# Expert rows turned by the DMA, pad rows written earlier, and dense rows loaded from ScalarE's queue

## The chip, the cores and the metric

The kernel runs on one core of one Trainium2 chip. The metric is the device time in microseconds (us), the median of three runs: 1864.76 us for the kernel before, with runs from 1861.49 to 1867.23. Lower is better. One further execution was profiled; it took 1854.92 us, of which the trace spans 1853.1 us.

## The reference, cut to what matters

One transformer layer, on x of 4 sequences of 1024 tokens with 256 features: latent attention with 16 heads, and then a mixture of experts beside a shared expert.

```python
x = x + attention(layernorm(x))               # 16 heads, causal, latent keys and values
h = layernorm(x)                              # the rest, per token of 4096
scores = softmax(h @ gate_w.T)                # 16 experts
topk_w, topk_idx = top_k(scores, 2)
combine = sum(one_hot(topk_idx) * topk_w)     # weights of the two experts of a token
gu = einsum('th,ehj->etj', h, w_gate_up)      # 2 x 176 columns per expert
y = einsum('eti,eih,te->th', silu(gate) * up, w_down, combine)
y = y + swiglu(h @ shared_gate_up) @ shared_down
x = x + y
```

A token needs only its two experts, so the kernel computes 8192 rows of expert work instead of 65536.

## The kernel before, in words

The 4096 tokens are 32 tiles of 128 rows. `section(t)` is the attention of tile t on every engine, t from 0 to 31, with side jobs of its neighbours between the units of the softmax: the projections of tile t + 2, the output projection of tile t - 1, and the shared expert and the router of tile t - 2. Two sections more (32 and 33) have no attention and finish the tiles 30 and 31. The order of the work on each engine is written out by hand (`SIDE`, `due`); engines meet at semaphores alone.

An operand of 32 bits is split into two f16 parts, high and low, and a product is three f16 products. So a row of an expert's input is 512 f16 numbers (256 high, 256 low).

The router picks two experts for each token. There is a list in HBM (`lists`) for each expert, and GpSimd scatters the normalized rows of a tile to the lists of their experts (`scatter`, two indirect DMAs per tile). A row of a list is 514 f16 numbers, 1028 bytes: the 512 of the input, and a 32-bit number that says to which row of `y_exp` the result belongs. `used` holds the next free row of each list; VectorE advances it in `places(q)`, and at the last tile it copies it to integers (`free_i`, semaphore `used_ready`).

A list does not end at a multiple of 128 rows, so pad rows are written behind each list: `write_pads` writes one tile of 128 pad rows at the free row of each of eight lists, once on SyncE (SP) and once on ScalarE (ACT), and SP writes one tile more to a dummy list. This is after section 33. SP then waits for the pads, for the scattered rows and for a table `tab`, which tells for each of 80 tiles of expert rows where it starts and whose it is.

The expert phase goes over these 80 tiles, eight in a round of the loop (`Fori`). For tile n, SP reads the start row into a register (`value_load`) and loads the tile into one of eight buffers (`xg`, semaphore `xg_in`). TensorE (PE) turns the four blocks of 128x128 with the identity (`xg_transposes`), ScalarE copies them from PSUM (`xg_copy`), PE multiplies with gate and up (`expert_up`), ScalarE and VectorE make the hidden rows, PE turns them (`h_transposes`), VectorE copies, PE multiplies with down (`expert_down`), ScalarE copies (`y_copy`) and GpSimd scatters the rows to `y_exp` (`send`). PE's order in step n is h_transposes(n), expert_up(n + 2), xg_transposes(n + 4), expert_down(n). SP loads tile n + 8 when the result of tile n has left (`m_out`), since the indices of the scatter lie in the same buffer.

Between its first eight loads and the loop SP also loads 4 MB of `dense`, the sum of x and the shared expert, for the last phase, in which VectorE adds the two weighted results of each token and the rows are stored.

SP issues in attention, too: the turns of queries, keys, outputs and hidden rows by DMA, the loads of x and the stores of `dense`. For section 32 these are, in this order, `load_residual(31)`, `turn_output(31, 1)` (half of the turned attention output of tile 31, which the output projection on PE waits for), `turn_hidden(30)`, `turn_x2(31)` and `store_dense(30)`.

Of the kernel before, what the change touches and what calls it, by code (L numbers as in the profile page):

```python
# [135 lines left out]
def build(nc, x, wqaT, wqb_peT, wqb_nopeT, wkva, wkT, wvT, wo, gateT, wgu, wd, wsg, wsd,  # L136
# [3 lines left out]
    with ctx:  # L140
# [3 lines left out]
        def sem(name):  # L144
# [105 lines left out]
                   m_xT m_xTs m_gu m_gate m_q m_hid m_hi m_lo m_hT m_hTs m_down m_y  # L250
# [10 lines left out]
        xg_in = [sem(f"xg_in{k}") for k in range(8)]  # L261
        m_out = [sem(f"m_out{k}") for k in range(8)]
# [59 lines left out]
        xg, w_at = carve(work, 0, (XB, ROW), F16)  # L322
        pT_mem = pT[:, 0, :, :, :].rearrange("p a g n -> p (a g n)").bitcast(F32)
        xgT, p_at = carve(pT_mem, 0, (2, 2, KD, P), F16)
        m_hs, p_at = carve(pT_mem, p_at, (2, 2, I_E), F16)
# [39 lines left out]

        def write_pads(eng, half):
            rows = nc.values_load_multi_w_load_instructions(free_i[0:1, half * E // 2:(half + 1) * E // 2],
                                                            engines=[eng.engine], min_val=0, max_val=DUMMY - P)[1]
            for row in rows:
                eng.dma_start(lists[ds(row, P), :], pad[:, :]).then_inc(s.pads, 16)  # L370
# [3 lines left out]
        def _(sp):  # L374
# [226 lines left out]
        def _(pe_):  # L601
# [231 lines left out]
            def xg_transposes(n, q, par, m):  # L833
                pe_.wait_ge(xg_in[q], m * 16 + 16)
                for a in range(2):
                    for k in range(KD):
                        last = pe_.transpose(tt[par][:, (2 * a + k) * P:(2 * a + k + 1) * P],  # L837
                                             xg[:, q, a * D + k * P:a * D + (k + 1) * P], id16[:, :])
                last.then_inc(s.m_xT, 1)

# [3 lines left out]
            def expert_up(n, par, e):  # L844
                pe_.wait_ge(s.m_xTs, n + 1)
                split_product(s_ps[:, par, 0:2 * I_E], lambda a, k: xgT[:, par, a, k, :],
                              lambda b, k: wgu_sb[:, k, ds(e, 1), b, :], list(range(KD))).then_inc(s.m_gu, 1)
# [30 lines left out]
            xg_transposes(0, 0, 0, 0)  # L878
            xg_transposes(1, 1, 1, 0)
            expert_up(0, 0, held_expert(0))  # L880
            xg_transposes(2, 2, 0, 0)
            expert_up(1, 1, held_expert(1))
            xg_transposes(3, 3, 1, 0)

            nc.disable_value_cache = False
            with pe_.Fori(0, NMT // XB - 1) as m:
                e = [held_expert(k) for k in range(3)]
                for q in range(XB):
                    n = m * XB + q
                    h_transposes(n, q % 2)  # L890
                    expert_up(n + 2, q % 2, e[q + 2])
                    if q + 3 < XB:
                        e.append(expert_of(n + 3))
                    else:

                        read_expert(n + 3, q + 3 - XB)
                        e.append(held_expert(q + 3 - XB))
                    xg_transposes(n + 4, (q + 4) % XB, q % 2, m + (q + 4) // XB)
                    expert_down(n, e[q])
            nc.disable_value_cache = True  # L900
            e = [held_expert(k) for k in range(3)]
            for q in range(XB):
                n = NMT - XB + q
                h_transposes(n, n % 2)
                if n + 2 < NMT:
                    expert_up(n + 2, n % 2, e[q + 2])
                if n + 3 < NMT:
                    e.append(expert_of(n + 3))
                if n + 4 < NMT:
                    xg_transposes(n + 4, (n + 4) % XB, n % 2, (n + 4) // XB)  # L910
                expert_down(n, e[q])
# [3 lines left out]
        def _(act):  # L915
# [193 lines left out]

            act.wait_ge(s.used_ready, 1)  # L1110
            write_pads(act, 1)


# [4 lines left out]

            def xg_copy(n, par):
                act.wait_ge(s.m_xT, n + 1)  # L1120
                copy(xgT[:, par, :, :, :].rearrange("p a k n -> p (a k n)"), tt[par][:, 0:4 * P]).then_inc(s.m_xTs, 1)
# [14 lines left out]
            xg_copy(0, 0)  # L1136
            xg_copy(1, 1)
            expert_gate(0, 0)
            xg_copy(2, 0)
            expert_gate(1, 1)  # L1140
            xg_copy(3, 1)
# [27 lines left out]
        def _(dve):  # L1169
# [203 lines left out]
            def places(q):  # L1373
# [153 lines left out]
            def section(t):  # L1527
                for k in range(units(t)):
                    side(t, k, 0)
                    prob_lo(t, k, 0)  # L1530
                    side(t, k, 1)
                    maxima_ahead(t, k)
                    prob_lo(t, k, 1)
                    if shifted(t % TB, k):
                        shifted_sums(t, k)
                    side(t, k, 2)
                    side(t, k, 3)
                    search(t, k)
                    if (t, k) == (4, 2):
                        expert_scales()  # L1540
                side(t, units(t), 0)
                search(t, "end")
# [4 lines left out]
            dve.memset(pad[:, 0:2 * D], 0.0)  # L1547
            dve.memset(pad[:, 2 * D:ROW].bitcast(I32), 2 * NY)
# [84 lines left out]
        def _(pool):  # L1633
# [70 lines left out]
            def scatter(q):  # L1704
# [60 lines left out]
            def send(n, q):  # L1765

                pool.wait_ge(s.m_y, n + 2)
                own_wait(pool)
                pool.indirect_dma_start(y_exp, bass.IndirectOffsetOnAxis(xg[:, q, 2 * D:ROW].bitcast(I32), 0), m_ys[:, q % YB, :],  # L1769
                                        None, bounds_check=NY - 1, oob_is_err=False).then_inc(m_out[q], 16)  # L1770
            with pool.Fori(0, NMT // XB) as m:
                for q in range(XB):
                    send(m * XB + q, q)
# [47 lines left out]
```

## Time and profile before

| | us |
|---|---|
| median of 3 runs | 1864.76 |
| the profiled execution | 1854.92 |
| its span in the trace | 1853.1 |
| attention sections, to the last output turn | 0 to 1546.9 |
| end of tiles 30 and 31 | 1546.9 to 1580.2 |
| pads, until the first load of expert rows | 1580.2 to 1596.7 |
| expert phase | 1596.7 to 1810.2 |
| combination | 1810.2 to 1853.1 |

Over the span PE is busy 84%, VectorE 71%, ScalarE 56% and GpSimd 53%. The share of an engine is a mean over these stages; what a change of one stage is worth is read from the rows of that stage. Times in the rows are us from the start of the span. "SPq" and "ACTq" are the sequencers of SP and ScalarE, on which DMAs are issued; the duration of a DMA row is what the issue took, and "to landing" runs from the issue to the completion. The names of buffers in the trace are those of the memory that they share: `xg` is `work`, the pad row is `x_sb`, `dense_sb` is `weights`, and `m_ys` is `probs`.

### The profile page before, as it was taken

To read this page: it belongs to the slowest core of one execution; us is meant where nothing else is said; L and a number is where in the kernel's file an instruction comes from. 1 tells how busy PE (TensorE), PEld (TensorE's weight loads), DVE (VectorE), ACT (ScalarE), POOL (GpSimd) and SP (SyncE) were. 2 spreads that over 40 slices of the span, in tenths; PEclk is the share of its full clock that TensorE was granted. 3 is DMA by queue.
4 is the path that set the end of the run, shared out by engine and by line. 5 is a ranking of instruction groups with operands and counts; after the bars stand their busy time and mean duration, and the time that the engine had idled before them with its cause. 6 is when DMAs were issued, how large, how long until landed. Compare 5 with 4: busy or idle time off the path is not lost.

```text
span 1853.1 us, 46010 instructions
## 1 busy us (share of the span) xinstructions
PE 1553.7 (84%) x16418; PEld 1100.7 (59%) x16419; DVE 1311.5 (71%) x2964; ACT 1028.9 (56%) x2344; POOL 978.4 (53%) x1580
## 2 busy tenths in 40 slices
PE   8765888999879999998799999888999995399980
PEld 3243566766656767666567666666667663266650
DVE  1365877788777877878687788768878884255556
ACT  1243565666656666665566666656666662266650
POOL 3024567655477776554777666557766423134440
PEclk9787899999999999999899999999999997699995
DMA  6337532212235333213533323234432111733327
GB/s 163 86 98 111 84 70 58 50 31 53 58 76 107 64 61 61 52 22 73 98 65 65 57 58 59 52 72 85 87 58 52 31 20 38 186 92 104 102 73 272
DMA packets 333653, 143.96 MB, mean 78 GB/s; under 512 B 277168, under 2 KB 328403, under 8 KB 333398
## 3 DMA queue, kind: packets, MB, share of 16 engines
q1 hardware_dynamic: 311584, 108.68, 29.5%
q10 hardware_dynamic: 14966, 15.88, 3.1%
q0 software_dynamic: 6912, 16.83, 2.7%
q8 instruction: 123, 2.02, 0.4%
q14 instruction: 68, 0.56, 0.1%
HBM read 46.78 MB, written 29.53 MB: 41 GB/s over the span
## 4 chain that ended last, share of the span: by engine, by line
PE 49%; DVE 20%; ACT 7%; issue 6%; DMA 5%; SPq 4%; POOL 3%; DVEq 1%; ACTq 0%; POOLq 0%
PE of_ps L603 23%; PE s_ps L603 14%; PE t_ps L759 10%; DVE pT L1485 5%; DVE smax L1456 3%; ACT pT L917 2%; SPq L427 2%; DVE smax L1460 2%; ACT probs L1041 1%; DVE nmax L1464 1%; DVE nmax L1467 1%; DMA y_exp<-probs,work 1%; DVE work L1291 1%; PE t_ps L837 1%; ACT probs L1046 1%
## 5 line engine op out<-in xcount | busy, mean ns | idle before, releaser
L1485 DVE TENSOR_TENSOR pT<-t_ps,pT 128x512 f16<-128x512 f32 (+3 forms) x688 | 409.7, 598 | 181.2 <-ACT pT L917 177.9
L917 ACT CAST pT<-t_ps 128x512 f16<-128x512 f32 (+3 forms) x688 | 354.6, 515 | 283.3 <-PE t_ps L759 282.1
L603 PE MATMUL s_ps<-kT,qT 128*128 128x512 f16 (+3 forms) x2304 | 491.9, 328 | 7.8 <-DMA kT<-ks_sb 4.3
L759 PE MATMUL t_ps<-id,probs 128*128 128x128 f32 x2304 | 382.9, 281 | 67.1 <-ACT probs L1041 26.6
L759 PEld LDWEIGHTS t_ps<-id,probs 128*128 128x128 f32 x2304 | 257.7, 142 | 167.9 <-issue 77.2
L1041 ACT ACTIVATE probs<-s_ps,nmax,fac 128x640 f32<-128x640 f32 (+3 forms) x256 | 269.1, 1051 | 1.9 <-DVE nmax L1464 1.9
L603 PE MATMUL of_ps<-weights,xT 128*128 128x512 f16 (+1 forms) x960 | 221.1, 370 | 56.6 <-DVE ks_sb L1280 22.5
L603 PEld LDWEIGHTS of_ps<-ckv,pT 128*128 128x128 f16 x6912 | 242.1, 98 | 43.0 <-DVE o_sb L1319 10.4
L603 PE MATMUL of_ps<-ckv,pT 128*128 128x64 f16 x6912 | 259.0, 194 | 8.0 <-DVE o_sb L1319 7.7
L603 PEld LDWEIGHTS s_ps<-kT,qT 128*128 128x128 f16 x2304 | 218.3, 99 | 76.1 <-issue 5.9
L603 PEld LDWEIGHTS of_ps<-weights,xT 128*128 128x128 f16 x960 | 83.3, 102 | 146.5 <-DVE ks_sb L1280 25.8
L1456 DVE TENSOR_REDUCE smax<-s_ps 128x1 f32<-128x512 f32 (+1 forms) x256 | 157.3, 648 | 4.1 <-PE s_ps L603 3.8
L1769 POOL DMA_INDIRECT y_exp<-probs,work x80 | 78.7, 984 | 148.9 <-ACT probs L1134 147.8
L1680 POOL TENSOR_TENSOR os_<-o_sb,os_ 128x512 f16<-128x512 f32 x60 | 70.1, 1168 | 161.7 <-ACT os_ L917 152.5
L1046 ACT ACTIVATE probs<-s_ps,nmax,fac 128x256 f32<-128x256 f32 (+3 forms) x224 | 144.2, 651 | 0.3 <-DVE nmax L1467 0.3
L1438 DVE TENSOR_REDUCE smax<-s_ps 128x1 f32<-128x768 f32 (+2 forms) x136 | 122.8, 903 | 12.8 <-PE s_ps L603 12.2
L603 PE MATMUL of_ps<-weights,oT 128*128 128x256 f16 x768 | 99.6, 292 | 25.1 <-DMA oT<-os_ 23.0
L1664 POOL TENSOR_TENSOR work<-work,sin_sb 128x544 f32<-128x544 f32 x60 | 95.2, 1586 | 45.9 <-ACT work L917 28.6
L603 PE MATMUL s_ps<-maskbf,idbf 128*128 128x128 bf16 x512 | 113.3, 221 | 0.0
L603 PEld LDWEIGHTS of_ps<-weights,oT 128*128 128x128 f16 x768 | 78.5, 104 | 43.0 <-issue 25.6
L1460 DVE TENSOR_REDUCE smax<-s_ps 128x1 f32<-128x512 f32 (+2 forms) x160 | 94.7, 627 | 5.6 <-PE s_ps L603 5.3
L603 PE MATMUL s_ps<-wgu_sb,pT 128*128 x480 | 86.8, 318 | 0.0
(210 smaller groups left out, 2428.8 us busy)
## 6 DMA issues: line engine op xcount, KB each, us to landing
work<-lists SPq DMA_DIRECT2D x80, 128.5 KB, 2.0
wgu_sb<-wgu ACTq DMA_DIRECT2D x2, 2816.0 KB, 10.9
x_sb<-x SPq DMA_DIRECT2D x32, 128.0 KB, 2.5
x<-x SPq DMA_DIRECT2D x32, 128.0 KB, 2.4
dense<-den SPq DMA_DIRECT2D x32, 128.0 KB, 2.7
weights<-dense SPq DMA_DIRECT2D x1, 4096.0 KB, 16.7
qT<-y_exp SPq DMA_DIRECT2D x16, 256.0 KB, 5.6
work<-y_exp SPq DMA_DIRECT2D x16, 256.0 KB, 7.0
```

Source lines behind the costliest of these rows:

```text
L603: return pe_.matmul(o, a, b, start=start, stop=stop)
L759: last = pe_.transpose(t_ps[:, h, c * P:(c + 1) * P], probs[:, u % 2, g * L + j * P:g * L + (j + 1) * P], id32[:, :])
L917: return act.copy(o, i)
L1041: act.activation(probs[:, par, 0:L], s_flat[:, 1024 * par:1024 * par + L], ACT.Exp, bias=nmax[:, par, 0:1], scale=f_att, accum_out=ssum[:, ...
L1046: last = act.activation(probs[:, par, g * L:(g + 1) * L], s_flat[:, base:base + L], ACT.Exp, bias=nmax[:, par, g:g + 1], scale=f_att, accu ...
L1438: dve.tensor_reduce(smax[:, par, 0:G], view, AX_X, ALU.max).then_inc(s.maxs, 1)
L1456: last = dve.tensor_reduce(smax[:, par, h:h + 1], bank[:, 0:(j1 - j0) * P], AX_X, ALU.max)
L1460: last = dve.tensor_reduce(smax[:, par, h * n:(h + 1) * n], view, AX_X, ALU.max)
L1485: dve.tensor_tensor(pT[:, u % 2, 1, h, 0:w], t_ps[:, h, 0:w], pT[:, u % 2, 0, h, 0:w], ALU.subtract).then_inc(s.lo_p, 1)
L1664: st_.do(pool.tensor_tensor(rot2[:, :, k:ROPE:2], pe_of(n)[:, :, 1 - k:ROPE:2], sin_b, ALU.mult))
L1680: pool.tensor_tensor(os_[:, 1, :], o_sb[:, :], os_[:, 0, :], ALU.subtract).then_inc(s.lo_o, 1)
L1769: pool.indirect_dma_start(y_exp, bass.IndirectOffsetOnAxis(xg[:, q, 2 * D:ROW].bitcast(I32), 0), m_ys[:, q % YB, :], None, bounds_check=NY ...
```

## The change

There are three parts.

- The rows of an expert tile come turned. SP issues a DMA transpose of 128 rows x 512 numbers out of `lists` in HBM into `xgT`, and a second DMA for the 4 bytes per row of the index (`m_rows`, new semaphores `rows_in`). `xg_transposes` on PE and `xg_copy` on ScalarE are gone. `expert_up` waits for `xg_in`, `send` for `rows_in`.
- The pads are written from the state after tile 29, in which a list may grow by at most 256 rows more, so that each list gets three tiles (384 rows) of pads. SP writes all of them, after its section 31. `free_i` is made in `places(29)`. The scatter of tile 30 on GpSimd waits until all pads have landed. VectorE makes the pad row at the start of section 30.
- `dense` is loaded from ScalarE's queue, ahead of its first `expert_gate`.

```diff
+        xgT, w_at = carve(work, 0, (XB, 2 * KD, P), F16)
+        m_rows, w_at = carve(work, w_at, (XB, 2), F16)
+        PADS = 3
             for row in rows:
-                eng.dma_start(lists[ds(row, P), :], pad[:, :]).then_inc(s.pads, 16)
+                eng.dma_start(lists[ds(row, PADS * P), :].rearrange("(p c) n -> p c n", c=PADS),
+                              pad.unsqueeze(1).broadcast_to([P, PADS, ROW])).then_inc(s.pads, 16)
 @block.sync
-            for t in range(NT + 2):
+            for t in range(NT):
                 section(t)
             sp.wait_ge(s.used_ready, 1)
-            write_pads(sp, 0)
+            for half in range(2):
+                write_pads(sp, half)
             sp.dma_start(lists[DUMMY:DUMMY + P, :], pad[:, :]).then_inc(s.pads, 16)
+            for t in range(NT, NT + 2):
+                section(t)
             def expert_rows(n, q):
                 row = sp.value_load(tab[0:1, 0, ds(n, 1)], min_val=0, max_val=DUMMY)
-                sp.dma_start(xg[:, q, :], lists[ds(row, P), :]).then_inc(xg_in[q], 16)
+                sp.dma_start_transpose(xgT[:, q], lists[ds(row, P), 0:2 * D]).then_inc(xg_in[q], 16)
+                sp.dma_start(m_rows[:, q, :], lists[ds(row, P), 2 * D:ROW]).then_inc(rows_in[q], 16)
-            for par in range(2):
-                sp.wait_ge(stored[par], 16 * NT // 2)
-            sp.wait_ge(s.side_made, JOB["down", NT - 1] + 1)
-            load(dense_sb, dense.rearrange("(t p) n -> p t n", p=P), s.dense_in)
 @block.tensor
-            def xg_transposes(n, q, par, m): ...
-            def expert_up(n, par, e):
-                pe_.wait_ge(s.m_xTs, n + 1)
+            def expert_up(n, q, m, e):
+                pe_.wait_ge(xg_in[q], m * 16 + 16)
-                    xg_transposes(n + 4, (q + 4) % XB, q % 2, m + (q + 4) // XB)
 @block.scalar
-            act.wait_ge(s.used_ready, 1)
-            write_pads(act, 1)
-            def xg_copy(n, par): ...
+            for par in range(2):
+                act.wait_ge(stored[par], 16 * NT // 2)
+            act.wait_ge(s.side_made, JOB["down", NT - 1] + 1)
+            load(dense_sb, dense.rearrange("(t p) n -> p t n", p=P), s.dense_in)
             expert_gate(0, 0)
-                if not last or n + 4 < NMT:
-                    xg_copy(n + 4, q % 2)
 @block.vector
-                if q == NT - 1:
+                if q == NT - 3:
                     dve.wait_ge(s.slot_s, 2 * q + 2)
                     dve.tensor_copy(free_i[:, :], used[0:1, :]).then_inc(s.used_ready, 1)
 @block.gpsimd
+                if q == NT - 2:
+                    pool.wait_ge(s.pads, 16 * (E + 1))
-            def send(n, q):
+            def send(n, q, m):
                 pool.wait_ge(s.m_y, n + 2)
+                pool.wait_ge(rows_in[q], m * 16 + 16)
```

On SP, the end of section 31 and the start of section 32 before: the store of dense rows of tile 29 (L393), the residual rows of tile 31 (L404) and the turns.

```order
L444 DMA_TRANSPOSE oT<-os_ 128x8x128 [waits side_made,lo_o]
L393 DMA dense<-den 128x256 [waits dense_done]
L404 DMA x<-x 128x256 [waits dense_done]
L444 DMA_TRANSPOSE oT<-os_ 128x8x128 [waits side_made,lo_o]
L451 DMA_TRANSPOSE hT<-hs 128x6x128 [waits side_made,lo_h]
L418 DMA_TRANSPOSE x2T<-xs 128x4x128 [waits side_made,ln2_done]
```

The same place now; of each eight pad writes one is shown:

```order
L448 DMA_TRANSPOSE oT<-os_ 128x8x128 [waits side_made,lo_o]
L397 DMA dense<-den 128x256 [waits dense_done]
L370 TENSOR_LOAD free_i [waits used_ready]
L370 ISA x16
L373 ISA
L373 DMA lists<-x_sb 384x1x514
...
L370 TENSOR_LOAD free_i
L370 ISA x16
L373 ISA
L373 DMA lists<-x_sb 384x1x514
...
L512 DMA lists<-x_sb 128x514
L408 DMA x<-x 128x256 [waits dense_done]
L448 DMA_TRANSPOSE oT<-os_ 128x8x128 [waits side_made,lo_o]
```

Sixteen writes of 384 rows and one of 128 now stand ahead of the residual load and of the last output turn.

On SP, one tile of the expert loop before:

```order
L517 ISA [waits m_out1]
L517 TENSOR_LOAD tab
L517 ISA x2
L518 ISA
L518 DMA work<-lists 128x514
L529 REGISTER_ALU
```

One tile of it now (L525 is the turned load, L526 the load of the indices):

```order
L524 ISA [waits m_out1]
L524 TENSOR_LOAD tab
L524 ISA x2
L525 ISA
L525 DMA_TRANSPOSE work<-lists 128x4x128
L526 ISA
L526 DMA work<-lists 128x2
L533 REGISTER_ALU
```

SP issues two DMAs per tile instead of one, and one of them is a transpose.

## Rows read from the trace of the kernel before

**Rows 1.** By stretch: us, PE, PEld, DVE, ACT, POOL busy, clock, DMA share, GB/s.

```profile
1609.50:1625.60 16.10, 9.19 (x71) 6.21 (x69) 5.10 (x15) 5.99 (x15) 3.92 (x4) 0.82 0.83 272
1625.60:1800.00 174.40, 162.41 (x1437) 112.78 (x1436) 97.78 (x288) 112.24 (x287) 70.81 (x72) 1.00 0.32 97
```

**Rows 2.** Timeline of PE and ScalarE in the expert loop: start, us, instruction.

```profile
1658.73 0.39 PE L854 MATMUL of_ps<-id,pT 128*88 128x128 f16 x4
1659.95 0.40 PE L837 MATMUL t_ps<-id,work 128*128 128x128 f16 x4
1660.32 0.84 PE L603 MATMUL of_ps<-wd_sb,work 88*128 x6
1661.00 0.39 PE L854 MATMUL of_ps<-id,pT 128*88 128x128 f16 x4
...
1660.05 0.41 ACT L1125 ACTIVATE gate<-s_ps,fac 128x176 f32<-128x176 f32 x1
1661.48 0.58 ACT L917 COPY pT<-t_ps 128x512 f16<-128x512 f16 x1
1661.95 0.48 ACT L1134 ACTIVATE probs<-of_ps,fac 128x256 f32<-128x256 f32 x1
1662.32 0.41 ACT L1125 ACTIVATE gate<-s_ps,fac 128x176 f32<-128x176 f32 x1
```

**Rows 3.** Chain of waits around the pads: start, us, what.

```profile
1577.19 0.72 SPq L367
...
1585.42 10.52 DMA lists<-x_sb
1596.70 0.36 SPq L518
```

**Rows 4.** SP's queue: expert loads without a wait, before the loop and in it.

```profile
1597.83 0.35 SPq L518 DMA_DIRECT2D work<-lists  x1
1598.98 0.34 SPq L518 DMA_DIRECT2D work<-lists  x1
...
1740.07 0.34 SPq L518 DMA_DIRECT2D work<-lists  x1
1741.42 0.34 SPq L518 DMA_DIRECT2D work<-lists  x1
```

**Rows 5.** Timeline of the last output turn and of what waits for it.

```profile
1528.16 0.48 DVE L1383 SCALAR_TENSOR_TENSOR den<-of_ps,fac,x 128x256 f32<-128x256 f32 x1
...
1546.93 1.24 SPq L444 DMA_TRANSPOSE oT<-os_  x1
...
1550.13 5.17 PE L603 MATMUL of_ps<-weights,oT 128*128 128x256 f16 x24 [2.24 <-DMA oT<-os_]
```

**Rows 6.** SP's queue: a turn, a store and a load back to back.

```profile
1300.89 1.19 SPq L411 DMA_TRANSPOSE xT<-xs  x1
1302.13 0.57 SPq L393 DMA_DIRECT2D dense<-den  x1
1302.76 0.42 SPq L404 DMA_DIRECT2D x<-x  x1
```

**Rows 7.** The chain's last step of the expert phase: start, us, what.

```profile
1807.55 2.12 DMA y_exp<-probs,work
```

**Rows 8.** GB/s moved in 40 slices of 1845 to 1853, stores of whole rows.

```profile
GB/s 343 353 358 133 20 0 0 0 0 0 154 353 353 348 103 0 0 0 0 0 0 159 369 348 338 98 0 0 0 0 0 0 205 348 348 338 72 0 0 0
```

**Rows 9.** GB/s moved in 40 slices of 1546 to 1551, the output turn alone.

```profile
GB/s 0 0 0 0 0 0 0 0 0 0 0 0 0 0 0 0 10 145 219 227 221 209 199 203 205 188 203 66 2 0 0 0 0 0 0 0 0 0 0 0
```

**Rows 10.** Pad writes: SP's issues in ns (min/median/max), and all to landing.

```profile
L370 SPq DMA_DIRECT2D lists<-x_sb x8: 333/480/724, 1580.2 to 1584.8; - x8
DMA to landing us min/median/max: 2.9/8.3/10.5
```

**Rows 11.** Last scatter to the lists, and scatters by the page: us to landing.

```profile
1580.01 0.96 POOL L1713 DMA_INDIRECT lists<-xs,slot  x1 [0.30 <-issue]
...
lists<-xs,slot POOLq DMA_INDIRECT x64, 3.1
```

More of the change, by code:

```diff
@@ L261, in build @@
         xg_in = [sem(f"xg_in{k}") for k in range(8)]
+        rows_in = [sem(f"rows_in{k}") for k in range(8)]
         m_out = [sem(f"m_out{k}") for k in range(8)]
@@ L321, in build @@
         os_mem = pT[:, 1, :, :, :].rearrange("p a g n -> p (a g n)").bitcast(F32)
-        xg, w_at = carve(work, 0, (XB, ROW), F16)
+        xgT, w_at = carve(work, 0, (XB, 2 * KD, P), F16)
+        m_rows, w_at = carve(work, w_at, (XB, 2), F16)
         pT_mem = pT[:, 0, :, :, :].rearrange("p a g n -> p (a g n)").bitcast(F32)
-        xgT, p_at = carve(pT_mem, 0, (2, 2, KD, P), F16)
-        m_hs, p_at = carve(pT_mem, p_at, (2, 2, I_E), F16)
+        m_hs, p_at = carve(pT_mem, 0, (2, 2, I_E), F16)
         m_hT_sb, w_at = carve(work, w_at, (2, 2, P), F16)
@@ L364, in build @@
         block = ctx.enter_context(nc.Block())
+        PADS = 3
         def write_pads(eng, half):
             rows = nc.values_load_multi_w_load_instructions(free_i[0:1, half * E // 2:(half + 1) * E // 2],
-                                                            engines=[eng.engine], min_val=0, max_val=DUMMY - P)[1]
+                                                            engines=[eng.engine], min_val=0, max_val=DUMMY - PADS * P)[1]
             for row in rows:
-                eng.dma_start(lists[ds(row, P), :], pad[:, :]).then_inc(s.pads, 16)
+                eng.dma_start(lists[ds(row, PADS * P), :].rearrange("(p c) n -> p c n", c=PADS),
+                              pad.unsqueeze(1).broadcast_to([P, PADS, ROW])).then_inc(s.pads, 16)
         @block.sync
@@ L831, in _ @@
             pe_.wait_ge(s.tab_ready, 1)
[L833 to L839, printed above, removed]
             def expert_of(n):
                 return pe_.value_load(tab[0:1, 1, ds(n, 1)], min_val=0, max_val=E - 1)
-            def expert_up(n, par, e):
-                pe_.wait_ge(s.m_xTs, n + 1)
-                split_product(s_ps[:, par, 0:2 * I_E], lambda a, k: xgT[:, par, a, k, :],
+            def expert_up(n, q, m, e):
+                pe_.wait_ge(xg_in[q], m * 16 + 16)
+                split_product(s_ps[:, q % 2, 0:2 * I_E], lambda a, k: xgT[:, q, 2 * a + k, :],
                               lambda b, k: wgu_sb[:, k, ds(e, 1), b, :], list(range(KD))).then_inc(s.m_gu, 1)
@@ L877, in _ @@
                 read_expert(n, n)
[L878 to L883, printed above, removed]
+            for n in range(2):
+                expert_up(n, n, 0, held_expert(n))
             nc.disable_value_cache = False
@@ L890, in _ @@
                     h_transposes(n, q % 2)
-                    expert_up(n + 2, q % 2, e[q + 2])
+                    expert_up(n + 2, (q + 2) % XB, m + (q + 2) // XB, e[q + 2])
                     if q + 3 < XB:
@@ L905, in _ @@
                 if n + 2 < NMT:
-                    expert_up(n + 2, n % 2, e[q + 2])
+                    expert_up(n + 2, q + 2, NMT // XB - 1, e[q + 2])
                 if n + 3 < NMT:
                     e.append(expert_of(n + 3))
-                if n + 4 < NMT:
-                    xg_transposes(n + 4, (n + 4) % XB, n % 2, (n + 4) // XB)
                 expert_down(n, e[q])
@@ L1540, in section @@
                         expert_scales()
+                    if (t, k) == (NT - 2, 0):
+                        dve.wait_ge(s.normed, NT)
+                        dve.memset(pad[:, 0:2 * D], 0.0)
+                        dve.memset(pad[:, 2 * D:ROW].bitcast(I32), 2 * NY)
                 side(t, units(t), 0)
@@ L1772, in _ @@
                 for q in range(XB):
-                    send(m * XB + q, q)
+                    send(m * XB + q, q, m)
 def kernel(**inputs):
```

13 lines of the change are left out of this document (2 added, 11 removed).

## The prediction, made before the changed kernel ran

> **What bounds the kernel now.** I read the busy time by stretch first, then the timelines inside the expert loop, then the chain of waits around the pads, and last SP's queue.
>
> In the steady part of the expert phase PE is busy 162.4 of 174.4 us at a granted clock of 1.00 (the upper level, 2.4 GHz), for 72 tiles: 2.42 us a tile [rows 1]. The reader sees in the timeline that a PE step starts every 1661.00 - 1658.73 = 2.27 us, and that ScalarE, too, goes round once in 1662.32 - 1660.05 = 2.27 us [rows 2]: both are full, and 0.15 us a tile is lost elsewhere, at the turn of a loop round above all. Ahead of it stands a stretch in which PE does nothing: from 1580.2 to 1596.7 the chain runs through the issue of pads and then 10.5 us of a pad write that lands last [rows 3]. A second hole lies in the stretch 1609.5 to 1625.6, PE busy 9.2 of 16.1 us at 272 GB/s of traffic, the load of the dense rows [rows 1].
>
> So there are three things to gain: PE and ScalarE work of a tile, the wait for pads, the collision with the dense load. Each is paid for on SP's queue, and I go through that.
>
> **1. PE and ScalarE in the expert loop.** The four transposes of a tile start 0.37 us ahead of the next product (1659.95 to 1660.32), the copy 0.47 us ahead of the next one (1661.48 to 1661.95) [rows 2]. Without them PE's round is 2.27 - 0.37 = 1.90 us, ScalarE's 2.27 - 0.47 = 1.80 us. With the 0.15 us of before they would do a tile in 2.05 us: 80 x (2.42 - 2.05) = 30 us less, if the rows come in time. The loads also have two steps more of slack: a tile is first wanted by expert_up(n + 2) and no longer by xg_transposes(n + 4).
>
> **2. SP in the expert loop.** A load costs SP its register work and its issue. Without a wait, loads follow each other by 1598.98 - 1597.83 = 1.15 us before the loop and by 1741.42 - 1740.07 = 1.35 us in it, of which 0.34 us is the issue [rows 4]. So 0.81 and 1.01 us are register work, which stays. The issue of 0.34 us becomes a transpose and a second DMA, with one more address calculation, for which I put 0.07 us (an estimate: two short register instructions). No row shows a transpose out of HBM. Its issue is bounded below by the plain read of the same rows, 0.34 us [rows 4], and above by 1.24 us, which the turn of twice the size took [rows 5]; the nearest row is the turn of exactly 128x512, 1.19 us, only out of SBUF [rows 6]. I take 1.19. The second DMA is between 0.34 [rows 4] and 0.57 us, which a store right behind a transpose took; a load in such a sequence took 0.42 [rows 6], and I take that.
>
> SP's round is then 1.01 + 1.19 + 0.07 + 0.42 = 2.69 us in the loop, 2.49 before it, and with 0.03 us a tile for the jump at the end of eight (an estimate) 2.72. That is more than the 2.05 us of PE and more than the 2.42 us of now: **SP becomes the bound of the expert phase.** The last of the 80 turned loads is issued 8 x 2.49 + 71 x 2.72 = 213 us after the first. Behind it come its landing, about 2.6 us (the turn of twice the size let PE start 3.2 us after its issue [rows 5]), and one pass through the engines: up, gate, hidden, turn, down, copy and the scatter's 2.1 us [rows 7], which I sum to 7.5 us. The results are all there 213 + 2.6 + 7.5 = 223 us after the first issue. Now it is 1809.7 - 1596.7 = 213 us [rows 3, 7].
>
> DMA engines don't bound this: their share is 0.32 [rows 1], and even with turns at half the rate of plain transfers they would stay under 0.6.
>
> At this place the Trainium skill says the opposite ("Advanced Engine Details and Errata", section "X-Bar Transpose (TRN2)"): transposing DMAs are as fast as regular ones. In this trace the turn out of SBUF moved 199 to 227 GB/s where stores of rows moved about 350, and its issue took 1.19 us against 0.42 [rows 6, 8, 9], so I don't follow it; what it would give is the first rival.
>
> **3. The pads.** They are not fewer: 16 x 3 + 1 = 49 tiles of 128.5 KB instead of 17. SP's first pad was issued at 1580.2, and the quickest landed 2.9 us after its issue, so at 1583.1; the last landed at 1585.42 + 10.52 = 1595.9 [rows 3, 10]: 16 in 12.8 us, 0.80 us each, or 0.71 if the two indirect scatters in flight at the time count as two more. The store of whole, aligned rows moves 350 GB/s [rows 8], 0.37 us for such a tile; that is the lower bound. I take 0.71: the same rows to the same lists.
>
> The state after tile 29 is known at about 1528.5 (its dense rows are made from 1528.16 [rows 5]). SP needed 3.0 us from reading the registers to the first issue (1577.19 to 1580.2 [rows 3, 10]), so the first write goes at 1531.6, lands at 1534.5, and the last at 1534.5 + 48 x 0.71 = 1568.6. Queued behind them on SP are the residual rows of tile 31, turn_output(31, 1) and turn_hidden(30). The output turn was issued at 1546.93 and let PE start at 1550.13 [rows 5]. Its 256 KB need 1.25 us at about 205 GB/s [rows 9], and the residual rows 0.4. So it lands at 1570 instead of 1550: **the end of tiles 30 and 31 is 20 us later.** With 0.37 us a tile it would be 1554, and 4 us later; with 0.80, 24 us. The output projection runs at the lower clock already (24 products in 5.17 us [rows 5]), so nothing more is lost there. The scatter of tile 30 waits for the pads, but it needs the output projection first, which is later than the pads. Nothing in section 31 uses SP after 1529 except these turns.
>
> That descriptors of one issuing engine are consumed in the order of its ring is what the Trainium skill states ("DMA: Bandwidth & Descriptors", section "Queues, rings and completion order"). The trace agrees as far as it goes: the last pad, of the same size as the others, landed 10.5 us after its issue where the first took 2.9 [rows 3, 10]. If turns could pass the pads, the delay would be near 0 and not 20.
>
> What is gained at the end of the stretch: nothing waits for pads there any more. The last scatter is issued at 1580.01 and takes 3.1 us [rows 11], and SP's first load followed its release by 1596.70 - 1595.94 = 0.8 us [rows 3]. So without the delay the first load would be issued at 1583.9 instead of 1596.7, 12.8 us earlier; with it at 1603.9, 7 us later.
>
> **4. The dense load on ScalarE's queue.** It is issued as soon as the last dense rows are stored, about when the first turned loads are, and runs some 12 us (4.2 MB at about 350 GB/s [rows 8]) beside five or six of them. They are issued every 2.5 us, so that sharing the engines costs latency and no rate. The hole at 1616 is gone, but where SP is the bound a hole of PE costs nothing. I put 0. If PE were the bound, the hole's 7 us would be gained; I have that in the first rival, since it counts no hole. Moving the pad row on VectorE costs nothing: it was made while PE waited for the output turn.
>
> **The sum.** The expert results are complete at 1583.9 + 20 + 223 = 1827 against 1809.7: +17 us. The combination is untouched. The profiled execution would be 1854.9 + 17 = 1872; the median of the runs stands 10 us above it, and I add the same 17 to that: **1882 us**.
>
> **Rivals.**
> - *The transpose out of HBM is issued as cheaply as a plain read* (0.34 us). SP's round is 1.01 + 0.34 + 0.07 + 0.42 = 1.84, below PE's 2.05. The phase is 2.6 + 79 x 2.05 + 7.5 = 172 us. Then 1583.9 + 20 + 172 = 1776, -34 us: 1831. For it: out of HBM a row is one run of memory, which no turn of this trace has as its source. Against it: turns of 128x512 and of 128x1024 differ by 0.05 us only [rows 5, 6], so that the cost seems to be that of the instruction. This is the rival on the other side; it decides from where SP's round falls below 2.50 us: the phase from the first issue is then 79 x 2.50 + 8.5 = 206 us, 7 us shorter than the 213 of now, which is what the late start takes. Chance 0.26.
> - *The same, and the pads are written at the rate of whole rows* (0.37 us): 4 us of delay, -50 us: 1815. Chance 0.08.
> - *SP is the bound, but the pads are fast*: 1583.9 + 4 + 223 = 1811, +1 us: 1866, no change that can be told. For it: three rows lie side by side for each partition. Chance 0.10.
> - *Everything on SP at its upper price*: 1.24 and 0.57 us make a round of 2.92, pads at 0.80: 8 x 2.69 + 71 x 2.92 + 10 = 239, and 1583.9 + 24 + 239 = 1847, +37 us: 1902. Chance 0.06.
>
> **Numbers.** The forecast has 0.50 and its own range is 1872 to 1896. About 0.3% (5.6 us) is what a measurement of this kernel can tell from no change. Faster: 0.26 + 0.08 and 0.02 of the third rival, 0.36. The same: 0.06. Slower: the rest, 0.58. The range goes from 1822, which leaves out the fast pads of the second rival, to 1898.
>
> **What would show it.** The turned load out of `lists` in SP's queue: an issue of about 1.2 us means the forecast, 0.3 to 0.5 the first rival. The distance between expert steps on PE: 2.7 us with waits of PE for the DMA of `work`, or 2.05 us without. The output projection of tile 31: its start at 1570 or near 1550. SP's issues should take a large share of the chain in the expert phase, where PE has it now. I am wrong if the turned loads are cheap, or if the turn of the output is not held by the pads.

## The result

The changed kernel takes 1902.64 us (median of 4 runs) against 1863.15 us of the kernel before (median of 4 on the same chip): it is slower, ratio 1.0198 with a 95% interval from 1.0164 to 1.0232. One of its four runs, at 1984.05 us, had a granted clock of 0.82 instead of 0.94 and is left out of the ratio; the median of the other three is 1900.96 us. The direction and the bound (SP in the expert phase) were forecast; the size was not: 1882 us was predicted, with a range up to 1898.

Stage by stage, from the two profiled executions (spans 1853.1 and 1894.9 us):

| stage | before | after | forecast |
|---|---|---|---|
| start to the store of `dense` of tile 29 | 1528.7 | 1534.2 | 1528.7 |
| from there to the output projection of tile 31 | 21.5 | 40.5 | 41.5 |
| from there to the first load of expert rows | 46.6 | 33.0 | 33.8 |
| first load to the last expert result in HBM | 213.0 | 244.4 | 223 |
| from there to the end | 43.4 | 42.8 | 43.4 |

The last column adds up from the working: 1550.13 + 20 - 1528.66 in the second row, 1583.9 - 1550.13 in the third, since the delay of 20 us is in both of its ends. In two rows the forecast is missed: the expert phase, by 21 us, and a first stage that no edit touches, by 5.5.

**The expert loop.** The stretch of SP's steady loop after; the columns are those of [rows 1].

```profile
1650.00:1840.00 190.00, 139.92 (x1042) 87.72 (x1039) 88.28 (x260) 73.04 (x195) 63.91 (x65) 1.00 0.35 83
```

PE was busy 162.4 of 174.4 us [rows 1] and is now busy 139.9 of 190.0 at the same granted clock of 1.00; 65 result scatters of GpSimd in 190 us make 2.92 us a tile, where it was 2.42. PE's timeline answers to [rows 2]:

```profile
1701.53 1.07 PE L607 MATMUL s_ps<-wgu_sb,work 128*128 x6
1702.72 0.84 PE L607 MATMUL of_ps<-wd_sb,work 88*128 x6
1703.40 0.39 PE L850 MATMUL of_ps<-id,pT 128*88 128x128 f16 x4
1704.85 1.07 PE L607 MATMUL s_ps<-wgu_sb,work 128*128 x6 [1.07 <-DMA work<-lists]
1706.02 0.84 PE L607 MATMUL of_ps<-wd_sb,work 88*128 x6
1706.70 0.39 PE L850 MATMUL of_ps<-id,pT 128*88 128x128 f16 x4
1707.66 1.07 PE L607 MATMUL s_ps<-wgu_sb,work 128*128 x6 [0.57 <-DMA work<-lists]
```

The transposes into `t_ps` are gone, and the first product of a tile waits for rows. In the page's list of line groups, whose part behind the bar reads busy us, mean ns of one and idle time ahead with its releaser, this product has 43.4 us of such waits; the next line is the scatter of the results:

```profile
L607 PE MATMUL s_ps<-wgu_sb,work 128*128 x480 | 88.9, 323 | 43.9 <-DMA work<-lists 43.4
L1754 POOL DMA_INDIRECT y_exp<-probs,work x80 | 78.7, 983 | 167.1 <-ACT probs L1115 157.7
```

SP's queue in the same stretch, which answers to [rows 4] (start, us that the issue took, line):

```profile
1702.06 1.22 SPq L525 DMA_TRANSPOSE work<-lists  x1
1703.47 0.42 SPq L526 DMA_DIRECT2D work<-lists  x1
1704.87 1.24 SPq L525 DMA_TRANSPOSE work<-lists  x1
1706.31 0.43 SPq L526 DMA_DIRECT2D work<-lists  x1
1707.84 1.22 SPq L525 DMA_TRANSPOSE work<-lists  x1
```

No row has a wait in front, and the view of SP's waits has none between 1632 and 1840 us: SP works all the time, 1704.87 - 1702.06 = 2.81 us for this tile and 2.97 for the next. Over the loop it is (1839.41 - 1630.64) / 71 = 2.94 us. The durations in ns over all 80 (min/median/max):

```profile
L525 SPq DMA_TRANSPOSE work<-lists x80: 782/1216/2576, 1607.7 to 1839.4; - x80
L526 SPq DMA_DIRECT2D work<-lists x80: 345/427/552, 1609.1 to 1840.8; - x80
```

The chain that ended last (each step followed back to what released it), in shares of the span: SP's queue has 14% of it, where it had 4%.

```profile
PE 39%; DVE 20%; SPq 14%; issue 8%; ACT 6%; DMA 4%; POOL 3%; DVEq 1%; ACTq 0%; POOLq 0%
```

**The pads.** SP's queue after the store of tile 29, which answers to [rows 5, 10]:

```profile
1534.19 0.33 SPq L397 DMA_DIRECT2D dense<-den  x1
1538.08 21.62 SPq L373 DMA_DIRECT2D lists<-x_sb  x16
1559.74 1.84 SPq L512 DMA_DIRECT2D lists<-x_sb  x1
1562.24 5.96 SPq L448 DMA_TRANSPOSE oT<-os_  x1
```

The time to landing of that last pad (L512) in this run:

```profile
DMA to landing us min/median/max: 14.0/14.0/14.0
```

The issue of the last pad in the kernel before:

```profile
1585.42 0.73 SPq L508 DMA_DIRECT2D lists<-x_sb  x1
```

And in the changed kernel the chain of waits from the output turn on, which answers to [rows 3]:

```profile
1562.24 12.29 DMA oT<-os_
1574.67 4.99 PE of_ps L607 x24
...
1604.20 2.64 DMA lists<-xs,slot
1607.67 1.21 SPq L525
```

The output turn is issued behind the last pad and the residual rows (a load of 0.51 us at 1561.63). Its issue alone takes 5.96 us where it took 1.24 [rows 5], and its data are there 12.29 us after it began, at 1574.5, where PE could start 3.2 us after it. The last pad had landed just before, at 1559.74 + 14.0 = 1573.7. So the turn's data come behind the pads', and SP itself is held while it issues; what holds it is not shown. The DMA engines were busy all this time (share 1.00 from 1534.2 to 1574.7), and no run puts the turn on a queue without pads: how much of the delay is the order in the queue and how much the shared engines stays open. The output projection starts 1574.67 - 1534.19 = 40.5 us after the store of tile 29, against 21.5. In the five other profiles with early pads it is 40.7 to 43.9 us.

### The profile page after: what moved, and what is told of

Its sections match the earlier page's. It is cut to its first block, busy times and chain, and to the rows that moved or that the text cites. A ratio compares the mean times of both kernels' runs of the same rounds, so it can differ in the third digit from the quotient of the medians.

```text
span 1894.9 us, 45449 instructions
## 1 busy us (share of the span) xinstructions
PE 1542.3 (81%) x16098; PEld 1083.6 (57%) x16099; DVE 1311.8 (69%) x2964; ACT 993.1 (52%) x2264; POOL 978.4 (52%) x1580
## 4 chain that ended last, share of the span: by engine, by line
PE 39%; DVE 20%; SPq 14%; issue 8%; ACT 6%; DMA 4%; POOL 3%; DVEq 1%; ACTq 0%; POOLq 0%
PE of_ps L607 19%; PE s_ps L607 11%; PE t_ps L763 10%; DVE pT L1464 6%; SPq L525 5%; DVE smax L1435 3%; ACT pT L906 2%; SPq L524 2%; DVE smax L1439 2%; SPq L526 2%; SPq L431 2%; DMA oT<-os_ 1%; ACT probs L1030 1%; DVE nmax L1446 1%; DVE nmax L1443 1%
## 5 line engine op out<-in xcount | busy, mean ns | idle before, releaser
L1417 DVE TENSOR_REDUCE smax<-s_ps 128x1 f32<-128x768 f32 (+2 forms) x136 | 122.8, 903 | 12.3 <-PE s_ps L607 11.4
L607 PE MATMUL s_ps<-wgu_sb,work 128*128 x480 | 88.9, 323 | 43.9 <-DMA work<-lists 43.4
L607 PEld LDWEIGHTS of_ps<-weights,oT 128*128 128x128 f16 x768 | 78.5, 104 | 60.5 <-issue 43.9
```

The costliest lines, as they stand in the source:

```text
L607: return pe_.matmul(o, a, b, start=start, stop=stop)
L1417: dve.tensor_reduce(smax[:, par, 0:G], view, AX_X, ALU.max).then_inc(s.maxs, 1)
```

## The experiments

Three sets, each with its own runs of the kernel before: 1866.89 us (21 runs), 1853.83 us (23 runs) and 1866.33 us (13 runs). The first has `a_pads_late`, `b_pads`, `b_dense` and `a_plain`; the second the three `a_batch` runs and `a_plain_v`; the third `b_order`, `a_pool` and `a_again`. These medians differ by 0.7%, so a run is compared by its ratio to the kernel before in its own set. Beside it I use a second measure, "behind attention": the span of the one profiled execution less the start of the store of `dense` of tile 29, since all edits but the making of the pad row on VectorE (at 1442 us) lie behind that. It is 324.4 us for the kernel before and 360.7 for the changed kernel.

**The changed kernel once more** (`a_again`, no edit).

> The changed kernel once more. Its attention, which no edit touches, ended 5.5 us later than in the profiled execution of the kernel before. Theory (this is spread from one execution to the next): the last stores ahead of the pads, at 1534.2 us there, fall anywhere from 1526 to 1539 us, and the time is 1.015 to 1.020 of the kernel before. Rival (the change itself slows attention, by its longer program or its other buffers): they come at 1534 us or later again.

1902.17 us (4 runs), ratio 1.0177 [1.0138, 1.0216]. The store came at

```profile
1540.47 0.33 SPq L397 DMA_DIRECT2D dense<-den  x1
```

which is even later than the theory allowed. That by itself would fit the rival. The profiles of each set say more. In the first set the same store comes at 1538.94 and 1538.07 us in the two variants of the kernel before, and at 1538.96 and 1535.47 in the two of the changed kernel: not later. In the third it comes at 1536.03 (`b_order`) against 1536.95 (`a_pool`) and 1540.47. In the second, whose kernel before is 12 to 13 us faster by its median, the four variants of the changed kernel have it at 1526.53 to 1530.41. So most of this spread lies between sets and the rest between executions, with no cause shown; an effect of the change of a few us on attention is not ruled out. Behind attention this run has 360.2 us and the first profile 360.7, 36 us more than the kernel before.

**The pads as before** (`a_pads_late`), and **the early pads alone** (`b_pads`).

```diff
 a_pads_late, against the changed kernel
-        PADS = 3
+        PADS = 1
-            for half in range(2):
-                write_pads(sp, half)
...
+            write_pads(sp, 0)            # after section 33
...
+            write_pads(act, 1)
...
-                if q == NT - 3:
+                if q == NT - 1:
```

GpSimd's wait for the pads goes with it. `b_pads` is the same edit in reverse, made to the kernel before. VectorE makes the pad row in section 30 in both.

> The changed kernel with the pads written as in the kernel before (one tile per list, after section 33, on both queues). Theory (SP is the bound of the expert phase, and the early pads hold the last output turn by 19 us while they save 13 us of waiting at the end): the output projection of tile 31 starts 19 us earlier, the first expert load comes 6 us earlier, SP's round stays at 2.8 to 2.9 us; in all -6 us, about 1897. Rival 1 (the early pads are free, the expert phase alone made the kernel slower): +13 us. Rival 2 (the early pads made most of the +39 us, by traffic as well): -25 us or more.

> The kernel before with the early pads of three tiles per list alone. Theory: the last output turn lands 19 us later, the wait for pads (13 us) is gone, the expert phase as before; in all +6 us, about 1869. Rival 1 (pads hidden behind attention): -13 us, about 1850. Rival 2 (traffic of pads slows more than the turn): +15 us or more.

`a_pads_late`: 1897.68 us, ratio 1.0184 [1.0165, 1.0202]; behind attention 356.6, 4 us less than the changed kernel, which the ratios (1.0198 and 1.0177 for that) can't tell. Its output projection starts 22.1 us behind the store and its first load 69.0 us (40.5 and 73.5 in the changed kernel), and the expert phase is 244.4 us as there. `b_pads`: 1873.02 us, ratio 1.0042 [1.0023, 1.0061]; behind attention 332.9, 8.5 us more than the kernel before. SP's queue in `b_pads`:

```profile
1538.94 0.33 SPq L396 DMA_DIRECT2D dense<-den  x1
1542.84 23.54 SPq L372 DMA_DIRECT2D lists<-x_sb  x16
1566.42 2.11 SPq L511 DMA_DIRECT2D lists<-x_sb  x1
1568.57 1.76 SPq L407 DMA_DIRECT2D x<-x  x1
1570.44 6.51 SPq L447 DMA_TRANSPOSE oT<-os_  x1
```

The same picture without turned expert rows. The early pads cost 4 to 8 us net (4.1 and 8.5 by single profiles, 0.42% or 8 us by the ratio of `b_pads`), the forecast had 7 (1603.9 against 1596.7).

**The dense load on ScalarE's queue alone** (`b_dense`).

```diff
 against the kernel before
-            load(dense_sb, dense.rearrange("(t p) n -> p t n", p=P), s.dense_in)     # SP
...
+            load(dense_sb, dense.rearrange("(t p) n -> p t n", p=P), s.dense_in)     # ScalarE
             xg_copy(0, 0)
```

> The kernel before with the dense load on ScalarE's queue alone. Theory: the 4 MB now move while the first expert tiles are loaded and before the first result is scattered, so that the hole of PE around 1616 to 1624 goes; the first loads land up to 3 us later; in all -4 us (0 to -7), about 1859. Rival (the hole moves to the first tiles in full): 0.

1863.38 us, ratio 0.9992 [0.9978, 1.0005], behind attention 321.8: nothing that the ratio can tell, where 4 us less were expected. The hole of PE in the loop is gone, and another has come at the start: SP issues the first loads at 1607.32 and 1608.46 us, but the rows of the second tile take 6.1 us.

```profile
1612.25 0.61 PE L833 MATMUL t_ps<-id,work 128*128 128x128 f16 x4 [20.49 <-DMA work<-lists]
1612.89 0.59 ACT L913 COPY pT<-t_ps 128x512 f16<-128x512 f16 x1 [16.57 <-PE t_ps L833]
1614.65 0.61 PE L833 MATMUL t_ps<-id,work 128*128 128x128 f16 x4 [1.79 <-DMA work<-lists]
```

**A plain load in place of the turned one** (`a_plain`). It decides whether the transposition or something else in the new load bounds.

```diff
 against the changed kernel
-                sp.dma_start_transpose(xgT[:, q], lists[ds(row, P), 0:2 * D]).then_inc(xg_in[q], 16)
+                sp.dma_start(xgT[:, q].rearrange("p a n -> p (a n)"), lists[ds(row, P), 0:2 * D]).then_inc(xg_in[q], 16)
```

The rows then lie unturned, so the results of this run and of the next are not the reference's; the two serve for timing alone.

> The changed kernel with the turned load replaced by a plain load of the same rows and bytes into the same buffer; the turn itself is left out. Theory (it is the issue of the transpose on SP, 1.22 us against 0.34, that bounds the phase): SP's round falls to about 1.95 us, PE is the bound at 2.05 to 2.15 us a tile, the phase is about 60 us shorter than the changed kernel's: about 1843. Rival (DMA engines, loop jumps or register reads bound it, not the transpose): less than 15 us are gained.

1861.32 us, ratio 0.9978 [0.9959, 0.9996]; behind attention 320.2, which is 40 us less than the changed kernel; the expert phase itself is 43.5 us shorter (1612.2 to 1813.1 against 1607.7 to 1852.1). The turned load is thus worth 40 us. The edit takes away the turn's issue and its data movement at once; that it is the issue follows from the queue above, in which SP never waits, and from `a_batch` below, which leaves the turned loads as they are and is 27 us shorter. My figure of 60 was too high, since PE's period did not fall to 2.05 us but to 2.1 to 2.3 in these rows:

```profile
1701.14 0.84 PE L607 MATMUL of_ps<-wd_sb,work 88*128 x6 [0.17 <-issue]
1701.82 0.39 PE L850 MATMUL of_ps<-id,pT 128*88 128x128 f16 x4
1702.05 1.06 PE L607 MATMUL s_ps<-wgu_sb,work 128*128 x6
1703.38 0.84 PE L607 MATMUL of_ps<-wd_sb,work 88*128 x6 [0.27 <-DVE work L1578]
```

VectorE in the same microsecond:

```profile
1702.56 0.34 DVE L1574 TENSOR_TENSOR pT<-x,pT 128x176 f16<-128x176 f32 x1 [0.40 <-issue]
1702.82 0.41 DVE L1578 COPY work<-of_ps 88x512 f16<-88x512 f16 x1
```

The output product waits for VectorE's copy of the turned hidden rows (L1578). PE had turned them at 1701.82 + 0.39 = 1702.21, but in VectorE's order the copy stands behind the lower parts of the next tile (L1574).

**The same with VectorE's copy ahead** (`a_plain_v`).

```diff
 against a_plain; VectorE's loop
                     hT_copy(n)
+                    expert_lo(n + 1, (q + 1) % 2)
                     expert_hidden(n + 2, q % 2)
```

`expert_lo` is the last step of `expert_hidden` (L1574), which now ends with its second product.

> The changed kernel with a plain load in place of the turned one (the rows are not turned, so what is multiplied is not the reference's), and VectorE's copy of the turned hidden rows ahead of the lower parts of the next tile. Without the second edit PE's period was 2.2 to 2.3 us, where its own work is 2.05. Theory (PE waits for VectorE's copy, which stands one operation late in VectorE's order): the period falls to about 2.1 us and 8 to 16 us come off, about 1850 us. Rival (ScalarE's and VectorE's chain through two tiles of 4.4 us sets it, wherever the copy stands): no change, 1861 us.

1838.1 us, ratio 0.9924 [0.9898, 0.995]; behind attention 308.0, 12 us less than `a_plain`. The late copy was on PE's path. Busy time of a stretch of the loop of `a_plain`, in the columns of [rows 1]:

```profile
1650.00:1780.00 130.00, 111.67 (x899) 73.54 (x897) 76.65 (x226) 63.58 (x170) 55.06 (x56) 1.00 0.39 107
```

And of `a_plain_v`:

```profile
1650.00:1770.00 120.00, 110.25 (x890) 72.77 (x888) 75.64 (x223) 62.32 (x167) 54.27 (x56) 1.00 0.41 113
```

The same 56 tiles take 130 us in the one and 120 in the other: 2.32 and 2.14 us a tile.

**The copy ahead in the kernel before** (`b_order`, the same edit there).

> The kernel before, with VectorE's copy of the turned hidden rows of tile n ahead of the lower parts of tile n+1. Theory (in the kernel before, PE is at its own work for 162.4 of 174.4 us of the expert loop, so at most 12 us of its waits can go, and part of these stand ahead of the output products): 3 to 8 us come off, about 1859 us. Rival: PE's rows are back to back there and its waits are those for rows at the jumps: no change.

1863.58 us, ratio 0.9993 [0.9977, 1.0008]; behind attention 324.4, as without it. The rival holds, with up to 4 us inside the interval. My reading is that with its own transposes PE has other work to do in the time in which the copy is late; no run tests it.

**Start rows read eight at once** (`a_batch`), **with late pads** (`a_batch_late`), **and with VectorE's copy ahead** (`a_batch_late_v`). This takes away a second part of SP's round.

```diff
 a_batch, against the changed kernel; a_batch_late and a_batch_late_v add the edits above
-                row = sp.value_load(tab[0:1, 0, ds(n, 1)], min_val=0, max_val=DUMMY)
...
+            def eight(first):
+                return nc.values_load_multi_w_load_instructions(tab[0:1, 0, ds(first, XB)], engines=[sp.engine],
+                                                                min_val=0, max_val=DUMMY)[1]
...
+                starts_ = eight(m * XB)
                 for q in range(XB):
...
+                    expert_rows(starts_[q], q)
```

> The changed kernel, but SyncE reads the eight start rows of a round at once, instead of one ahead of each load. Theory (SyncE bounds the expert phase, and about 1.0 of its 2.94 us a tile is the reading of the address): about 0.34 us of register work is left per tile, SyncE's round falls to some 2.3 us, the phase to some 195 to 205 us: about 1860 us, 42 below the changed kernel, and PE waits for other engines in the expert loop more than for the rows. Rival (the loads queue behind each other, so their work and not SyncE's issue sets the rhythm): less than 10 us gained, SyncE's turned load starting as seldom as before.

> The same with the pads as in the kernel before (one tile per list, after the last output turn, half of them on ScalarE's queue). Theory: the pads' 6 us come off as they did with the slower rows, about 1855 us, 0.995 of the kernel before. Rival: with SyncE faster, the first rows now start early enough for the pads to be on the path again, and the gain is nothing.

> The same as the one before, and VectorE copies the turned hidden rows of tile n ahead of the lower parts of tile n+1 instead of behind them. Theory: if SyncE's round is still over 2.25 us, SyncE bounds and nothing changes (within 3 us); only if it is below, PE's period falls with the earlier copy. Rival: PE's period is set by this copy already, and 8 to 16 us (0.1 to 0.2 a tile) come off.

`a_batch` 1865.21 us, ratio 1.0068 [1.0045, 1.0091], behind attention 334.0; `a_batch_late` 1856.39 us, 1.0013 [0.9995, 1.003], 325.8; `a_batch_late_v` 1855.9 us, 1.001 [0.9993, 1.0028], 324.6. SP's queue of the last, over the end of a round of eight:

```profile
1714.05 1.19 SPq L527 DMA_TRANSPOSE work<-lists  x1
1715.44 0.43 SPq L528 DMA_DIRECT2D work<-lists  x1
1716.16 1.19 SPq L527 DMA_TRANSPOSE work<-lists  x1
1717.55 0.44 SPq L528 DMA_DIRECT2D work<-lists  x1
1721.22 1.21 SPq L527 DMA_TRANSPOSE work<-lists  x1
```

Inside a round a tile takes 2.11 us, and the step to the next round, with its eight reads, 5.06: (7 x 2.10 + 5.06) / 8 = 2.47 us a tile where it was 2.94. 80 x 0.47 = 38 us would be the whole effect, 27 came (360.7 - 334.0; by the ratios 20 to 24). The phase is 30.3 us shorter (1607.5 to 1821.6), and the first load came 3.6 us later behind the store. I had expected 2.3 and 42 us: the reads did not shrink to nothing, eight at once with the jump of the loop still cost 5.06 - 2.10 = 3.0 us. The late pads took off 8.2 us more, where 6 were expected, but the 0.995 that I expected of `a_batch_late` did not come, since `a_batch` had fallen short. While SP's round is 2.47, VectorE's earlier copy is worth 1.3 us behind attention and nothing that the ratio shows, as its theory said; with the plain loads, where SP is out of the way, the same edit gave 12.

**The index loads on GpSimd's queue** (`a_pool`, all edits so far and this one).

```diff
 against a_batch_late_v
-                sp.dma_start(m_rows[:, q, :], lists[ds(row, P), 2 * D:ROW]).then_inc(rows_in[q], 16)
+                pool.dma_start(m_rows[:, q, :], lists[ds(row, P), 2 * D:ROW]).then_inc(rows_in[q], 16)
```

GpSimd issues it four tiles ahead of the result's scatter, and reads its start rows four at once.

> The changed kernel with late pads, start rows read at once and VectorE's earlier copy, and the loads of the index column on GpSimd's queue instead of SyncE's. Theory (SyncE's round is 2.47 us with its index load, 0.62 of it that load and the work ahead of it): SyncE falls to 1.85 us a tile and PE bounds at 2.1 to 2.2, so some 25 us come off, about 1830 us. Rival: a plain load costs GpSimd about 1 us, as its indirect stores do, and with them and its registers GpSimd's round is over 2.5 us: slower than 1856 us.

1848.88 us (4 runs), ratio 0.9893 [0.9866, 0.992]; behind attention 312.1. This version beats both kernels, the one before by 1.1% and the changed one by 2.8% (0.9893 / 1.0177 = 0.972, both ratios of one set). By the ratios of the two sets it is 22 us better than `a_batch_late_v` (1.001 to 0.9893), but behind attention 12.5 us (324.6 - 312.1), and 12.3 us or 0.7% better than the kernel before. The two measures don't agree here; the rest of the 1.1% lies ahead of the store or in the spread of four runs. The theory's 25 us are not shown. The index load costs GpSimd 0.56 us of issue and not the rival's 1 us (columns: ns min/median/max):

```profile
L1771 POOL DMA_DIRECT2D work<-lists x80: 534/565/602, 1608.2 to 1793.4; - x80
```

In the loop, by the columns of [rows 1], PE is busy 116 of 130 us, with 58 of GpSimd's pairs of DMAs, or 2.24 us a tile:

```profile
1650.00:1780.00 130.00, 116.03 (x920) 76.34 (x917) 78.49 (x231) 64.44 (x174) 91.15 (x116) 0.99 0.46 110
```

SP is no longer the bound: in these 130 us PE waits 2.9 us for rows, and SP itself waits for a free buffer, 9.7 us from 1640 to 1790. What keeps the period at 2.24 us, where `a_plain_v` has 2.14, was not tried; GpSimd is now busy 91 of 130 us, without its register work.

## Why the forecast had the right sign and the wrong size

- **The turned load out of HBM is as dear as one out of SBUF: right.** Forecast 1.19 us by the nearest row [rows 6], measured 1.22. `a_plain` shows that the turned load is worth 40 us of time. The first two rivals (0.34 us) fall, and with them what the Trainium skill states ("Advanced Engine Details and Errata", section "X-Bar Transpose (TRN2)": transposing DMAs as fast as regular ones): for the issue on SP it doesn't hold here, 1.22 us against 0.34 [rows 4]. How fast the data of such a turn move out of HBM was not measured apart.
- **SP becomes the bound of the expert phase: right.** PE waits 43 us for rows, SP's loads follow each other with no wait. Each thing taken off SP's round (transposition, register reads, index load) made the kernel faster (40, 27 and 12 us behind attention); taking PE's wait off by VectorE's order did not while SP was slower.
- **SP's round is 2.72 us: wrong, this is the step that failed.** Measured 2.94. The index load was right (0.42 and 0.43), the register work before a transposition as well (1.01 and 0.98). But the second address calculation, which I estimated at 0.07 us, takes 0.19. That is 0.12 of the 0.22 us that are missing. The chain shows its pieces between the end of one issue (1833.79 + 1.23) and the next:

```profile
1833.79 1.23 SPq L525
1835.01 0.04 issue
1835.06 0.05 SPq L526
1835.10 0.04 issue
1835.15 0.03 SPq L526
1835.17 0.03 issue
1835.21 0.43 SPq L526
```

  Two register instructions, 0.08 us, and around them 0.11 us in which nothing is shown. A DMA at a constant address follows a turn at once: 1302.13 - 1302.08 = 0.05 us [rows 6]. So 1.22 + 0.19 + 0.43 + 0.98 = 2.82, which is the usual distance in the trace. The rest of the 2.94 are the step at the end of eight (3.2 to 3.5 us each, on average 0.06 a tile and not 0.03) and single slow steps, 0.06 a tile: most up to 3.1 us, and one of 4.34 with an issue of 2.58. Why these are slow is not shown, and no row had stood behind the 0.07 and the 0.03.
- **The phase is 223 us: 21 too short.** 71 x (2.94 - 2.72) = 15.6 of it are the loop's round. The first eight rounds took 2.64 each and not 2.49, and the load of tile 8 came 1.9 us late, 1.2 of them a wait for its buffer: 1630.64 - 1607.67 = 23.0 against 19.9, 3.1 us. From the last issue to the last result it took 12.7 us and not 10.1, 2.6 us. The sum is 21.3. The fourth rival had a similar round (2.92) and the right total, but by other prices: 0.57 for the index load and 1.24 for the transposition, neither of which is what was measured.
- **The pads hold the output turn by 20 us: right.** 40.5 - 21.5 = 19.0. I took 0.71 us for 128.5 KB; from the first landing (1538.08 + 4.3) to the last (1573.7) it is 0.65. Against that the first write was issued 3.9 us after the store and not 2.9, and took 4.3 us to land and not 2.9: that the sum is right to 1 us is in part luck. `b_pads` shows the hold in a kernel without turned rows, 21.9 us. The Trainium skill ("DMA: Bandwidth & Descriptors", section "Queues, rings and completion order") has the descriptors of a ring consumed in the ring's order; the trace agrees as far as it goes, since the turn (1574.5) was not there before the last of the 17 writes ahead of it (1573.7). That SP itself is held in its issue (5.96 us for the turn) was not foreseen; I see no cost of it here.
- **The wait for pads at the end goes: right.** 33.0 us from the output projection to the first load, forecast 33.8. The net of both is 5.4 us here (19.0 - 13.6) and 8.5 in `b_pads`.
- **The dense load on ScalarE's queue is worth 0: right as far as it was tried.** It was not tried apart in the changed kernel. With PE as the bound, where I had put 7 us, `b_dense` gained nothing that its ratio shows and 2.6 us behind attention.
- **PE's 2.05 us a tile in the first rival: wrong.** It came from taking PE's transposes off its period. They had hidden that the output product waits for VectorE's copy. With a cheap load it is some 2.3 us a tile (130 / 56 = 2.32): `a_plain` ends 0.2% below the kernel before, and the forecast of the rival was 1.8%.
- **Attention was taken as fixed.** It came 5.5 us later in the profiled run. That weighs little in the times: the kernel before was profiled in an execution of 1854.92 us, faster than all its timed runs (1861.49 to 1867.23), and the medians differ by 37.8 to 39.5 us, near the 36.3 behind attention. The miss is the expert phase. The range had no room for the round's upper bounds, though the text had bounds of 0.57 and 1.24 us in it that alone make 2.92. The upper end should have been the fourth rival's 1902 at least.
- **Three readings of the working were off, with little weight.** ScalarE was called full, but it was busy 112.2 of 174.4 us [rows 1]. The landing after 2.9 us was that of ScalarE's first pad; SP's first took 4.1. And the threshold of 2.50 us for SP's round was worked out with a tail of 8.5 us, where the forecast has 2.6 + 7.5 = 10.1; with that it is 2.48.

## What to carry to other kernels

Moving work from an engine to DMA moves it to the queue that issues the DMA: count that engine's round with every issue, every register read and every address calculation, and take 0.2 us and not 0.07 for the address of a second DMA if it lies in a register, as measured here, and leave room in the range for uneven steps. When one engine gets work taken off, ask which waits this work had covered: with cheap loads the next bound was not the engine's own 2.05 us but 2.32, and 2.14 once an operation that stood one place late in VectorE's order was moved. Spread the issues of a loop over the engines that wait in it, and read the registers for several steps at once.

## What was not expected of the hardware

- Reading a start row from SBUF into a register and using it costs SP 0.98 us a tile inside a round, 1.04 with the jump's share, and 0.65 us with eight read at once, jump included (3.0 / 8 + 0.28).
- A plain DMA of 0.5 KB issued by GpSimd took 0.56 us against 0.43 on SP.
- Behind 6.3 MB of pad writes the issue of a turn took 5.96 us instead of 1.24, and that of the last pad 1.84 instead of 0.73. So writes that are still under way can hold the engine that issues; the plain load between the two took only 0.51.
- The same code, but for the pad row on VectorE, ended anywhere from 1526.5 to 1540.5 us in thirteen profiled executions, 14 us apart; within a set of runs they are 3.5 to 5.5 us apart. A difference of a few us between two profiles is better measured from the last point that both kernels reach by the same instructions.
